# Sharing the weighted sum of routed results between VectorE, ScalarE and GpSimd

## The reference

```
out[token] = x[token] + sum over k < K of weight[token, k] * y[token, k]     (256 channels)
```

## Time and profile before

| | |
|---|---|
| time, median of 3 runs | 2118.67 us (2117.53 to 2118.79) |
| profiled execution, its own time | 2134.49 us |
| its span in the trace | 2132.7 us |
| VectorE in the weighted sum of layer 1 | 495.65 to 521.07 us |
| VectorE in the weighted sum of layer 3 | 2115.54 to 2129.40 us |

### The profile page before, as it was taken

One profiled execution on the slowest core, in us unless ns is written; L12 is line 12 of the kernel. 1 busy time (PEld: TensorE's weight loads), 2 busy tenths in 40 slices (PEclk: granted clock), 3 DMA queues, 4 the chain that ended last, 5 costly groups with the idle time before them and its releaser, 6 DMA issues. The chain is left out here.

```text
span 2132.7 us, 36972 instructions
## 1 busy us (share of the span) xinstructions
PE 1835.4 (86%) x13816; PEld 1446.0 (68%) x13816; DVE 1396.8 (65%) x2980; ACT 736.7 (35%) x1729; POOL 569.7 (27%) x550
## 2 busy tenths in 40 slices
PE   5953479990899999999999996989997997989995
PEld 2341257770799989998999995455566885767773
DVE  4477255556787777778787876566656778544444
ACT  2222334440333433333334333135534323322231
POOL 1234615551021222212121211632323102511111
PEclk9975569995899999999999998999997996999998
DMA  8419324436000000000000100000001007111114
GB/s 312 145 48 295 117 81 152 136 112 221 1 2 24 2 24 1 24 24 1 24 1 24 33 1 1 1 1 2 2 1 53 28 1 247 60 38 50 51 46 140
DMA packets 102876, 134.74 MB, mean 63 GB/s; under 512 B 11568, under 2 KB 78796, under 8 KB 102192
## 3 DMA queue, kind: packets, MB, share of 16 engines
q1 hardware_dynamic: 91616, 101.89, 15.2%
q0 software_dynamic: 11088, 30.49, 4.0%
HBM read 81.80 MB, written 50.54 MB: 62 GB/s over the span
## 5 line engine op out<-in xcount | busy, mean ns | idle before, releaser
L1119 POOL TENSOR_TENSOR a_rstd<-a_msq,consts 128x8 f32<-128x8 f32 x32 | 52.4, 1637 | 554.1 <-DVE a_msq L1474 554.1
L110 PE MATMUL a_ring<-a_w_hi,l_xnT_hi 128*128 128x256 f32 x512 | 152.0, 297 | 0.0
L110 PE MATMUL a_ring<-a_w_hi,l_xnT_lo 128*128 128x256 f32 x512 | 144.5, 282 | 0.0
L110 PE MATMUL a_ring<-a_w_lo,l_xnT_hi 128*128 128x256 f32 x512 | 144.3, 282 | 0.0
L2468 POOL DMA_INDIRECT l_slots_in<-xn,f_row_of x96 | 98.0, 1021 | 95.1 <-DVE f_row_of L2796 37.0
L3029 POOL DMA_INDIRECT l_pairs_out<-f_yb,f_to_row x96 | 95.6, 996 | 101.1 <-ACT f_yb L3004 69.5
L1431 DVE RECIPROCAL a_rT<-a_rT 128x256 f32<-128x256 f32 x64 | 111.5, 1743 | 0.0
L1720 PE MATMUL b_ring<-b_keys,b_qm 32*128 32x128 f32 (+2 forms) x896 | 91.5, 340 | 14.9 <-DVE b_nm L1933 9.4
L1886 ACT ACTIVATE b_work<-b_ring 128x1024 f32<-128x1024 f32 (+1 forms) x96 | 81.0, 881 | 62.3 <-PE b_ring L1727 61.3
L2923 PE MATMUL f_pgu<-f_gate_up_w,f_xT 128*128 x384 | 95.4, 392 | 6.2 <-ACT f_xT L2984 5.5
L110 PEld LDWEIGHTS a_ring<-a_w_hi,l_xnT_hi 128*128 128x128 f32 x512 | 97.5, 190 | 0.2 <-issue 0.2
(11 more groups left out here) (507 smaller groups left out, 5404.7 us busy)
## 6 DMA issues: line engine op xcount, KB each, us to landing
l_slots_in<-l_zeros SPq DMA_DIRECT2D x4, 3120.0 KB, 22.3
f_xb<-l_slots_in SPq DMA_DIRECT2D x11, 1040.0 KB
f_gate_up_w<-l_pairs_out SPq DMA_DIRECT2D x16, 512.0 KB, 8.8
l_slots_in<-l_zeros SPq DMA_DIRECT2D x3, 1690.0 KB, 18.6
f_xb<-l_slots_in SPq DMA_DIRECT2D x39, 130.0 KB, 2.0
f_down_w<-L_ffn_w_down_dram SPq DMA_DIRECT2D x1, 4096.0 KB
f_gate_w<-L_ffn_w_dram SPq DMA_DIRECT2D x2, 2048.0 KB, 10.5
f_up_w<-L_ffn_w_dram SPq DMA_DIRECT2D x2, 2048.0 KB, 19.7
```

Of the source, the lines that this page charges most:

```text
L110: ins = pe.matmul(out, a, b, start=start and k == 0, stop=stop and k == 2, **kw)
L1119: pool.tensor_tensor(rstd[:], msq[:], core.consts[:, C_HALF:C_HALF + 8], ALU.pow).then_inc(s["rstd_ready"], 1)
```

## The change

In groups 1 to 6 of both layers, VectorE keeps only the even tile. The odd tile's K results are multiplied by their weights in place by ScalarE (K instructions of 128x256), then summed by GpSimd in halves (for K = 4 one sum of 128x512 and one of 128x256, for K = 2 one of 128x256) and added to x by GpSimd (one more of 128x256). Groups 0 and 7 stay VectorE's alone. ScalarE's and GpSimd's new parts stand at the end of their programs. In layer 3 SyncE's stores of a shared group wait for GpSimd's semaphore too; in layer 1 the block's end does that. In layer 1 GpSimd also waits for `bias_added`, which is raised at the block's beginning.

```
+SHARED = (1, 2, 3, 4, 5, 6)
+
+def own_tiles(g):
+    return (2 * g,) if g in SHARED else (2 * g, 2 * g + 1)
+
+def added_up_to(r, g):
+    return r.K * sum(len(own_tiles(i)) for i in range(g + 1))
+
 def add_pairs(dve, core, r, landed, back_in, added):
     for g in range(GROUPS):
         dve.wait_ge(back_in[g], 32)
+        tiles, before = own_tiles(g), added_up_to(r, g - 1)
         for k in range(r.K):
-            for t in (2 * g, 2 * g + 1):
+            for n, t in enumerate(tiles):
                 if k:
-                    dve.wait_ge(added, 2 * r.K * g + 2 * (k - 1) + t % 2 + 1)
+                    dve.wait_ge(added, before + len(tiles) * (k - 1) + n + 1)
                 dve.scalar_tensor_tensor(out=core.x[:, t, :], in0=landed[:, t, k, :], scalar=r.weight[:, t, k:k + 1],
                                          in1=core.x[:, t, :], op0=ALU.mult, op1=ALU.add).then_inc(added, 1)
+
+def weigh_shared(act, r, landed, back_in, weighed):
+    for g in SHARED:
+        act.wait_ge(back_in[g], 32)
+        for k in range(r.K):
+            rows = landed[:, 2 * g + 1, k, :]
+            ins = act.activation(rows, rows, ACT.Copy, scale=r.weight[:, 2 * g + 1, k:k + 1])
+        ins.then_inc(weighed, 1)
+
+def sum_shared(pool, core, r, landed, weighed, halved, summed):
+    steps = Steps(pool, halved)
+    for n, g in enumerate(SHARED):
+        t = 2 * g + 1
+        pool.wait_ge(weighed, n + 1)
+        half = r.K // 2
+        while half:
+            steps(pool.tensor_tensor(landed[:, t, 0:half, :], landed[:, t, 0:half, :], landed[:, t, half:2 * half, :],
+                                     ALU.add))
+            half //= 2
+        pool.tensor_tensor(core.x[:, t, :], core.x[:, t, :], landed[:, t, 0, :], ALU.add).then_inc(summed, 1)
...
 (slots_experts)
+            weigh_shared(act, r, landed, back_in, s["weighed"])
...
+            pool.wait_ge(s["bias_added"], 2 * STRIPS)
+            sum_shared(pool, core, r, landed, s["weighed"], s["halved"], s["summed"])
...
 (slots_experts3, SyncE)
             for g in range(GROUPS):
-                sp.wait_ge(s["added"], 2 * K * (g + 1))
+                sp.wait_ge(s["added"], added_up_to(r, g))
+                if g in SHARED:
+                    sp.wait_ge(s["summed"], SHARED.index(g) + 1)
...
+            sum_shared(pool, core, r, landed, s["weighed"], s["halved"], s["summed"])
...
+            weigh_shared(act, r, landed, back_in, s["weighed"])
```

More of the change, by code:

```diff
@@ L2874, in slots_experts @@
     names = ("x_turned x_copied gu_ready setup_step limits_ready biased clipped silu_ready h_ready h_turned h_copied "
-             "y_ready y_copied rows_step rows_found cw_turned cw_copied bias_ready bias_added added").split()
+             "y_ready y_copied rows_step rows_found cw_turned cw_copied bias_ready bias_added added weighed halved summed").split()
     s = {n: sem(n) for n in names}
@@ L3107, in slots_experts3 @@
     px, ph, py = st.ps("px", [P, 512]), st.ps("ph", [P, 512]), st.ps("py", [P, 2, 512])
-    names = ("x_turned x_rounded x_split x_copied gate_ready up_ready silu_ready h_ready h_turned h_copied y_ready y_copied rows_step rows_found added").split()
+    names = ("x_turned x_rounded x_split x_copied gate_ready up_ready silu_ready h_ready h_turned h_copied y_ready y_copied rows_step rows_found added weighed halved summed").split()
     s = {n: sem(n) for n in names}
```

## The result

The changed kernel takes 2124.43 us (median of 9 runs, 2120.84 to 2127.20) against 2117.53 us of the kernel before in the same runs (2114.53 to 2118.99): ratio 1.0029, 95% interval 1.002 to 1.0038. It is 6.1 us slower by the ratio (4.2 to 8.0 by its interval), 6.9 by the medians. 5.5 was forecast, and 2124.2.

What follows compares the result with a forecast made beforehand. Two stretches, ending layers 1 and 3, were taken as bound almost equally by VectorE's additions and load landings. Losses of 3.7 and 1.8 us sum to 5.5, on 2118.67 making 2124.2 us; range 2117.5 to 2130.

Steps and rivals of the forecast that it cites:

- Taking turns: Shared groups, both layers: GpSimd's sums and VectorE's additions alternate, one addition per sum; +3.7 and +1.8 us; chance 0.50.
- The rival that takes its "fully blocks" to the whole duration: Both layers: nothing overlaps, whole durations add up; +9.3 us in layer 1, +5.1 in layer 3, 2133.1 together; chance 0.17.
- without contention: Both layers: GpSimd and VectorE do not hold each other up; -1.2 us in layer 1, 0 in layer 3, 2117.5; chance 0.13.
- with more turns: Both layers: VectorE gets more than one turn between sums; +1.2 us in layer 1, +1.1 in layer 3, 2121.0; chance 0.20.
- The two terms for the additions: VectorE's end in layer 1 later by 3.7 us, the last stores of layer 3 issued later by 1.8.
- 0.195: Shared groups: us by which each VectorE addition between two sums lengthens GpSimd's chain.
- 0.325: Shared groups: us after a GpSimd sum's end at which VectorE's held addition ends, 0.475 less 0.15 hidden.
- 0.13: Shared groups: us before VectorE's end from which GpSimd's next, held sum counts as started.
- ScalarE's weighing: Shared groups: 0.38 us per 128x256 weighing, anything from 0.30 to 0.45 allowed, keeping up with the loads and not felt.
- the block ends behind layer 1 are the same barrier: Between layer 1's last addition and the next layer: same barrier as before, so no change forecast there.
- the base: The kernel before: median 2118.67 us of three runs, to which the forecast loss was added.
- The ceilings that the landings were said to leave: Ends of both stretches: given when the last loads land, at most 1.2 us to gain in layer 1, 0.8 in layer 3.

Runs made afterwards that it cites:

- Experiment 2: The changed kernel with GpSimd's sums, and the stores' wait for them, left out in both layers; ratio 0.9995 to the kernel before.
- 3: The changed kernel with VectorE's running sum of a tile kept in PSUM until the last addition writes x; ratio 1.0031 to the kernel before.
- experiment 1: The changed kernel with one more GpSimd drain before its sums, in both layers; ratio 1.0020 to the kernel before.
- experiment 4: The kernel before, with GpSimd in layer 1 waiting for the last group to land and then writing four unused columns; ratio 1.0010 to the kernel before.

## Why the prediction was right, and where its sum was not

**Taking turns** was right, and in its form: one addition for each sum, eighteen in layer 1. Experiment 2 shows that the sums are the cause, 3 that it is the second input in SBUF, which is the rule of the Trainium skill (SBUF — State Buffer, Who interferes with whom): a VectorE instruction with two SBUF inputs contends with a GpSimd one that reads SBUF. The rival that takes its "fully blocks" to the whole duration would have put VectorE's end 9.3 us late; it was 2.8. What each keeps is measured: a held addition ended 0.28 us behind GpSimd's sum (482.51 against 482.23), so 0.20 of its 0.48 was hidden. The rivals without contention and with more turns fell too: VectorE's end would have been 1.2 sooner, or 1.2 later.

**Sizes.** The two terms for the additions were both too large: layer 1 +2.8 instead of +3.7, layer 3 +0.7 at the end instead of +1.8. A group of GpSimd's took 3.13 us instead of 3.3, and a pair of sums in layer 3 1.73 instead of 1.84: one addition between two sums lengthened GpSimd's chain by 0.14, not by 0.195. Most of that is the 0.28 behind GpSimd's end, for which the sum had 0.325; GpSimd's next sum counts from 0.14 to 0.15 before VectorE's end (483.06 + 1.44 - 1.27 against 483.37), not far from the 0.13 assumed. That 0.13 was itself misread: the earlier trace rows have GpSimd's held sum start at 87.2, not 87.27, which gives 0.2. The 0.7 of layer 3 is of one execution; that of experiment 1 has 1.1. In layer 3 groups 1 and 2 also met no full row of turns: VectorE waited for their loads and had three of its four additions there undisturbed. ScalarE's weighing took 0.49 us in place of the 0.38 of the earlier trace rows, outside of what I allowed (0.45), and was not felt.

**The step that failed** is "the block ends behind layer 1 are the same barrier". The barrier is the same, 1.75 us behind the last engine to come and 1.78 before; what changed is when GpSimd comes to it. By giving GpSimd work behind its indirect DMAs, the change moved its end-of-block drain, 7.9 us long, from under the loads to behind the sums, and 3.4 us of it stuck out. I had followed the queues for what stands behind a wait, but not what the block's end makes each engine do, because the views of busy time don't show it. Two terms too large by 0.9 and 1.1 and one of 3.4 left out make 6.9 of 5.5. So the mechanism of the additions was right, but that the time was met, 2124.4 against 2124.2, is luck: errors of opposite sign nearly made up for each other, and the base was 1.1 lower in nine runs than in the three.

The ceilings that the landings were said to leave were right for layer 1 (1.2 named, 1.1 in experiment 2) and wrong for layer 3, where 0.8 was named and nothing came: there SyncE's 32 issues follow each other without a gap from 0 to 18.1. Whether its issues or the DMA engines (359 GB/s in the earlier trace rows) hold that row back was not separated.

## What to carry to other kernels

Before moving elementwise work from VectorE to an idle GpSimd, count VectorE's instructions with two SBUF inputs in that stretch: here each sum held one of them, and a group shared cost VectorE 0.6 us more than it saved. Keep one of the inputs in PSUM if a bank is free; here the two engines then ran side by side, at 0.48 us an addition.

A last instruction on GpSimd had a price of its own here, because GpSimd had sent indirect DMAs in the block (four columns written cost 3.7 us at the block's end in experiment 4): look at the drains at the block's end. Put a drain ahead of work appended behind such DMAs, in time that is idle anyway. And first ask what the sharing could give at best: with the last group left whole, the loads left 1.1 us here.

## What the runs showed of the hardware that was not expected

In three blocks GpSimd's drain took 0.083 us, behind GpSimd's last work, for each indirect DMA (128 rows each) sent since the last drain: 7.92 us for 96, 5.30 for 64, 3.97 for 48, 3.26 for 39, and 0.1 when a drain came between. It is paid when the drain comes, even 29 us after the last of those DMAs was sent (experiment 4). Two shorter ones do not fit: in layer 3's routing a drain behind 4 of them took 1.7 to 1.9 us and one behind 28 took 2.7 to 3.1, over all the traces, more than 0.083 each. What a drain works off, and whether it goes by the DMAs or by their rows, was not tried.

A VectorE addition of 128x256 with both inputs in SBUF took 0.83 to 0.95 us when a 128x256 sum held it and 1.37 to 1.48 when a 128x512 sum did; with one input in PSUM it kept 0.48 to 0.49 beside 128x256 sums, whether it wrote PSUM or SBUF, and a 128x512 sum that started beside such an addition kept 1.26 (1.44 beside one with both inputs in SBUF).
